# Four-block GNN on one core: which engine scales the second iteration of a walk's slot by the inverse counts

## The reference

```python
h = jnp.maximum(_layernorm(x, axis=-1), 0.0)
# block 3, _L2_gnn_ref
deg = jnp.clip(segment_sum(ones, col), 1.0)[:, None]
for _ in range(6):
    agg = segment_sum(x[row], col)
    message = (agg / deg) @ W_h_weight.T + W_h_bias
    x = x + relu(message)
# block 4, _L3_gnn_ref: a gcn convolution, tanh, and a product with W2
```

## Time and profile before

| | us |
|---|---|
| three runs, median | 3777.04 |
| lowest and highest | 3771.08, 3794.89 |
| span of the profiled execution | 3778.5 |
| busy in it: TensorE | 2654.6 (70%) |
| VectorE | 2151.6 (57%) |
| ACT | 2009.2 (53%) |
| GpSimd | 1431.0 (38%) |

### The profile page before, as it was taken

How to read it: one execution, slowest core, us unless ns; L and a number is a source line. 1 busy time by engine, 2 the same in 40 slices (tenths; PEclk the granted TensorE clock), 3 DMA queues, 4 the chain that set the end, 5 groups by cost and what they waited for, 6 DMA issues and landing times. The chain is left out here.

```text
span 3778.5 us, 45814 instructions
## 1 busy us (share of the span) xinstructions
PE 2654.6 (70%) x11055; PEld 1615.7 (43%) x11055; DVE 2151.6 (57%) x7980; ACT 2009.2 (53%) x4381; POOL 1431.0 (38%) x1507
## 2 busy tenths in 40 slices
PE   4666555656666667799999747787787878775641
PEld 2433333434544545554444322454454545443420
DVE  5533254556658856433333466677677777776620
ACT  1555455556556665455555488565666566553400
POOL 5444434442534335100000000546464645444476
PEclk8877777778888888999999858888889888876865
DMA  4544343344445555334334388444454444333210
GB/s 87 148 132 125 103 119 100 95 121 124 123 128 177 165 150 168 123 133 137 135 136 136 128 259 291 136 144 143 133 160 137 152 143 153 120 106 101 82 58 37
DMA packets 528965, 504.90 MB, mean 134 GB/s; under 512 B 58706, under 2 KB 389955, under 8 KB 528616
## 3 DMA queue, kind: packets, MB, share of 16 engines
q1 hardware_dynamic: 477388, 415.73, 34.4%
q0 software_dynamic: 47184, 85.73, 8.7%
q10 hardware_dynamic: 4172, 0.99, 0.1%
HBM read 246.45 MB, written 260.27 MB: 134 GB/s over the span
## 5 line engine op out<-in xcount | busy, mean ns | idle before, releaser
L1839 POOL DMA_INDIRECT h_G<-step_tab,row_i x294 | 282.0, 959 | 470.3 <-DMA step_tab<-l_NR 194.1
L796 PE MATMUL a_PA<-a_H,w 128*128 128x512 f32 x504 | 308.6, 745 | 197.7 <-ACT a_H L960 160.8
L1839 POOL DMA_INDIRECT h_M<-step_tab,row_i x294 | 283.8, 965 | 227.1 <-PE h_P L1944 148.0
L1559 DVE TENSOR_SCALAR b_Y<-b_BP,col 128x512 f32<-128x512 f32 x148 | 109.9, 743 | 354.2 <-PE b_BP L1513 354.2
L1513 PE MATMUL b_BP<-b_Z,w 128*128 128x512 f32 x592 | 266.3, 592 | 0.0
L270 POOL DMA_INDIRECT h_G<-msg_tab,row_i x147 | 142.1, 967 | 318.4 <-PE h_P L306 150.8
L1541 ACT ACTIVATE b_Z<-b_BQ,bn 128x512 f32<-128x512 f32 x148 | 115.0, 777 | 257.2 <-PE b_BQ L1505 256.9
L208 ACT ACTIVATE l_ln_sd<-l_ln_mv,lneps 128x8 f32<-128x8 f32 (+1 forms) x136 | 41.0, 301 | 383.1 <-DVE l_ln_mv L2149 219.6
L2185 DVE TENSOR_TENSOR_SCAN h_T<-keep,h_T,h_P 128x512 f32<-128x512 bf16 x196 | 223.3, 1139 | 35.7 <-issue 18.6
L796 PEld LDWEIGHTS a_PA<-a_H,w 128*128 128x128 f32 x504 | 105.9, 236 | 322.1 <-ACT a_H L960 191.5
L969 ACT ACTIVATE a_H<-a_PA,col 128x512 f32<-128x512 f32 x252 | 163.7, 669 | 140.0 <-PE a_PA L796 87.8
(11 more groups left out here) (384 smaller groups left out, 6730.5 us busy)
## 6 DMA issues: line engine op xcount, KB each, us to landing
b_HI<-hin_tab SPq DMA_DIRECT2D x148, 256.0 KB, 2.8
y_tab<-b_Y SPq DMA_DIRECT2D x148, 256.0 KB, 2.0
l_Y<-y_tab SPq DMA_DIRECT2D x148, 256.0 KB
l_X<-x_tab SPq DMA_DIRECT2D x148, 256.0 KB
x_tab<-a_X SPq DMA_DIRECT2D x112, 256.0 KB
hin_tab<-a_HI SPq DMA_DIRECT2D x112, 256.0 KB
a_XR<-in_x SPq DMA_DIRECT2D x97, 256.0 KB
out_rows<-l_O SPq DMA_DIRECT2D x97, 256.0 KB
```

Of the source, the lines that this page charges most:

```text
L796: nc.tensor.matmul(PA[b][:, 0:nt * P], w[:, :], h[b][:, 0:nt, :].rearrange("p t d -> p (t d)"), start=True, stop=True).then_inc(done, 1)
L1559: nc.vector.tensor_scalar(Y[b][:, :], BP[b][:, :], col[:, C_B12:C_B12 + 1], None, ALU.add).then_inc(b_y, 1)
L1839: pool.indirect_dma_start(out=GR_[i % 2][b][:, k, :], out_offset=None, in_=table[:, :], in_offset=bass.IndirectOffsetOnAxis(ap=row_i[:, t ...
```

## The change

In the second iteration of each walk slot (`its[1:]`, walks only, `i < F0`), the two VectorE instructions of `affine` are taken out. ACT does the same product instead, tile by tile: seven activations of 128x128 with Relu, the inverse counts as scale, from `h_P` to `h_Z`. They stand in ACT's list behind `norm1(j)` and ahead of `pn.act_std` and `ln2.act_std(j)`. `update` takes the maximum with 0 as before, which a Relu ahead of it does not alter. The first iteration of a slot stays on VectorE.

```diff
--- before.py
+++ after.py
@@ -2061,6 +2061,17 @@
                     rows = ZR[i % 2][b][:, 0:nt, :]
                     nc.scalar.activation(rows, rows, AF.Tanh, bias=col[:, C_B31:C_B31 + 1]).then_inc(f_th, 1)
 
+            def scale_rows(i):
+
+                for b in range(2):
+                    n, t, nt = hop_at(i, b)
+                    act.wait_ge(wk_prod, n + 1)
+                    act.wait_ge(wk_out, n - 1)
+                    for k in range(nt):
+                        last = nc.scalar.activation(Z[b][:, k, :], PH[b][:, k * P:(k + 1) * P], AF.Relu,
+                                                    scale=inv_cnt[:, t + k:t + k + 1])
+                    last.then_inc(wk_z, 1)
+
             z(0)
             late = None
             for place, sl in enumerate(slots):
@@ -2092,6 +2103,8 @@
                         ln2.act_std(act, j - 1 - MIX)
                         norm2(j - 1)
                 for i in its[1:]:
+                    if i < F0:
+                        scale_rows(i)
                     if LASTW < i < F0:
                         pn.act_std(act, i - LASTW - 1)
                 if j is not None and is_d(j):
@@ -2274,9 +2287,7 @@
                 if j is not None and is_d(j):
                     stats2(j)
                 for i in its[1:]:
-                    if i < F0:
-                        affine(i, 0)
-                    else:
+                    if i >= F0:
                         end_scale(i)
                     if LASTW < i < F0:
                         end_rstd(i - LASTW - 1)
@@ -2284,7 +2295,6 @@
                     rstd2(j)
                 for i in its[1:]:
                     if i < F0:
-                        affine(i, 1)
                         update(i)
                     if LASTW <= i < F0:
                         end_stats(i - LASTW)
```

## The result

The changed kernel takes 3836.9 us (median of four runs, 3827.02 to 3852.12) against 3778.67 us for the kernel before, runs taken beside one another: ratio 1.0158, 95% interval 1.0123 to 1.0192. It is slower by 58 us. The profiled execution has a span of 3844.4 us, 65.9 more than that of before.

A forecast was written before the change was run, and what follows sets the result against it. The prediction took a two-slot chain through the root, norm2 and gather bursts as the bound. Terms of 21 + 4 + 8 + 2 + 4 us, less 5, added 34 to 3778.5; adjusted to the median, 3811, stated as 3810, range 3758 to 3868.

The forecast's parts named there:

- likeliest case: Walk slots: the path grows by half the root's delay in each slot; 3811 us, range 3785 to 3835, chance 0.50.
- second rival: ACT's list becomes a ring, so each slot pays the root's delay whole: 3850 us, chance 0.20.
- d/2 = 0.6 us for one: The chain through norm2 grows by the root's delay over two slots, so 0.6 us per slot, 21 us over 35.
- the prediction's chain: Path over two slots through affine, update, scan, root, norm2, TensorE's turn and two gather bursts: 44.25 us, 22.1 per slot.
- Part 1: VectorE loses two instructions; the one between rstd2 and update brings update and the next x2 0.45 us earlier.
- Part 2: Seven activations on ACT ahead of the root, spaced 0.27 to 0.36 us, take 1.9 to 2.5 us.
- Part 3: The root's table load on ACT moves behind the seven Relus, where nothing hides it: 1.28 us.
- Delay d: How much later the root starts in the 34 slots: mean 0.85 to 1.5 us, taken as 1.2.
- last sentence: The forecast fails above all if TensorE's signals are held at other times once their order against the bursts changes.
- Part 4: Sum over all walks: 21 + 4 + 8 + 2 + 4 = 39 us slower, less 5, so 34.
- 21 + 4 + 4, less 5: 35 slots 21 us, ends of walks 4, held products 4; less 5 for slots where norm2 had room.
- Third and fourth rival: Third: bursts alone set the slot, 3770 to 3785, chance 0.15; fourth: bursts may start earlier, 3735 to 3770, chance 0.15.

The follow-up runs named there:

- the second group behind the root: Changed kernel with ACT scaling only the second group (3 tiles), behind the root, and VectorE the first: 3296.83 us, ratio 1.007 to the kernel before.
- the early load's run with the first group: Changed kernel with a one-column dummy root on ACT before the scaling, and only the first four tiles scaled there: 3269.87 us, ratio 0.9987 to the kernel before.

## Why the prediction was right or wrong

The forecast was 3810, the range 3758 to 3868; the time of 3837 is in it. The direction, the place of the load and the price of the load and of the work were right. The loss, 58 us, was forecast as 33 (3810 less 3777). That lies above the likeliest case's own range, 3785 to 3835, and is held by the range only because the second rival's 3850 was let in: the forecast of each slot's growth, 0.6 us, was well under half of the 1.6 measured.

- **What bounds the slot.** That the root and `norm2` are on the path is confirmed by the second group behind the root: half a microsecond between root and `norm2` costs 24 us. That the chain runs over two slots, by way of the gather bursts, is one step that failed ("d/2 = 0.6 us for one"). In the changed kernel the ring closes in one slot, through TensorE's list, on both chips: TensorE is idle for 0.04 us a slot between `prod` and the last `hop_prod` on the first chip and not at all on the quiet one, and in both `turn2` then waits 3.1 us for `norm2`. The list was read (its order stands ahead of the prediction), but not that it has no gap there, nor that on the quiet chip the root hangs on `x3`, which stands in front of `hop_prod` in it. For the kernel before on the first chip the prediction's chain is not refuted: its slots are 2.4 us longer there than on the quiet chip, with TensorE idle for 0.54 us in that stretch. The second rival said "paid whole in each slot"; its result was near (3850), its mechanism was another: ACT's list is not the ring, as the 168 activations more in the early load's run with the first group show.
- **Part 1**, 0.45 us on the path: `update` did come directly behind `rstd2`, but it is worth nothing where `norm2` is the bound.
- **Part 2**, 0.27 to 0.36 us apiece: 2.01 us for seven, so 0.27 from one to the next; 366 ns for one. At the lower bound. Cost of the work without the load: 13 us.
- **Part 3**, the table load moves behind the scaling: right, and the largest term, 73 of 86 us where it could be measured. Its 1.28 us was sized rightly, what it is worth was not: 38 x 1.28 is 49, and the rest is TensorE's lower clock, a term that the prediction did not have. The Trainium skill's rule (ScalarE: Activation LUTs, "Table sets: the hidden batching unit") that a load is put before an activation that needs one is what the rows show: 2089.99, behind seven Relus, and 2317.84, behind a mere wait. Of the drain of about 1.38 us that the Trainium skill adds to a load (ScalarE: Activation LUTs, "What ACT_TABLE_LOAD costs") the rows show nothing again: load at 2089.99, root at 2091.29.
- **Delay d**, 0.85 to 1.5 us, taken as 1.2: this is the other step that failed. Root behind moments is 1.66 us on average on the quiet chip and 2.85 on the first. The prediction counted held products in 3 of 35 slots and gave them 2 to 4 us each; after the change the second product is seen over 0.5 us late in 23 of 35, in 13 of them 7.1 to 7.2 us behind the start of a burst, and not at 10.0 to 10.3. Its last sentence had named this as the way to fail. Half of 2.85 over 35 slots would be 50 us, near the 55 measured in walks one to five, so the first chip's numbers alone would not have told a halved large delay from a whole small one; the traces of TensorE do.
- **Part 4.** Walks one to five: 55 us against 24 (21 + 4 + 4, less 5). Last walk: 9.6 us against 10. Ends of walks are in the walk figures and can't be told apart.
- **Third and fourth rival.** Bursts did not set the changed kernel's slot, and in the slot shown no burst starts right behind the one ahead of it: 2474.35, 1.94 us behind 2472.41, though TensorE had turned the first four tiles at 2470.57. The turn's signal is still held.

## What to carry to other kernels

A table load is placed at the instruction that needs it, so anything put ahead of that instruction, even an empty wait, can bring a hidden load onto the path; a one-column dummy of the same function in idle time puts it back. To price a delay, look for the shortest ring that closes through an engine's list without idle time, here TensorE's from `prod` to `hop_prod`; only a longer ring dilutes it. A delay that leaves TensorE idle longer can cost twice, once on the ring and once by the granted clock of the work behind it. An engine with 40% idle time is no place for free work if the work stands in front of the one small instruction that another engine waits for.

## What the runs showed of the hardware

- TensorE's signals are held back while a burst of seven indirect gathers is under way, on the two chips with 3779 and 3725 us and not on the three with 3272 to 3273, with the same program: the second `affine` of the first iteration starts 3.25 us late in the earlier trace rows and directly behind its product in the trace with 3277.48 us. ACT's signals of the same microseconds are not late: 8.2 us into a burst TensorE's turn starts at 2472.11, 0.15 us behind the last activation (2471.96). What holds them was not found; a kernel without half of the gathers, which could tell, was not tried.
- Four short matmuls a slot in TensorE's idle time raise the granted clock of the walks from 0.88 to 0.94 and shorten the kernel before by 35 us on one chip; with ten a slot the changed kernel, 0.85 without them on the first chip, has 0.96.
- With the same work of TensorE, its granted clock in the walks is 0.93 in the kernel before and 0.87 in the changed one on the quiet chip, where `turn2` waits 3.07 us a slot in place of 0.60, and one `prod` matmul takes 1028 ns in place of 897.
- The stages ahead of the walks take some 375 us more on the first chip than on a quiet one (first scan of the walks at 2380 us against 2005) and 312 more on the chip with 3725 (2317), with equal work. It concerns both kernels alike.
